# Begin of block attention: order of batch 1's rows, place of the value sums, and added products on TensorE

## Chip, core and metric

The kernel runs on one NeuronCore of one Trainium2 chip. The metric is the device time of one execution in microseconds (us); before the change the median of 3 runs is 1207.91 (1207.45 to 1208.69). Engines: PE is TensorE, DVE is VectorE, ACT is ScalarE, POOL is GpSimd, and SP issues most DMAs.

## The reference, cut to what matters

Four stages with residuals follow one another on x of shape (2, 1024, 128): a 16-head rotary attention, a routed layer of 8 experts, a block attention (16 heads of 8 features), and a gated mixing layer. The change lies at the border of the second and third stage.

```
x = x + experts(layernorm(x))                      # end of it: rows fetched back, added to x
h = layernorm(x)                                   # block attention
q, k, v = h @ Wq.T + bq, h @ Wk.T + bk, h @ Wv.T + bv     # 16 heads of 8
scores = q . k / sqrt(8);  where block(key) > block(query) the score is 0, not -inf   # blocks of 32
probs = softmax(scores);   ctx = probs @ v;        x = x + ctx @ Wo.T + bo
```

Since keys of later blocks have the score 0 and not minus infinity, they keep a weight in the softmax. The kernel adds their part with sums of v over later blocks ("suffix" sums).

## The kernel before

Each stage is a `Block`: five instruction streams, one for each engine, in an order written out by hand, with semaphores between them. A block ends when all five streams have ended, and the next one begins some 0.3 us later.

**End of `experts`.** SP fetches the sorted results back in four loads (`fetched[0..3]`). VectorE adds them to x, two loads first, then takes layer norm statistics of batch 0 and the variance (`var_ready`), then adds the other two loads. ACT takes the root. PE has no work after the last expert product.

**Projection block (inner block of `block_attention`).** Rows are normalized on VectorE (`take_rstd`, `normalize_rows`), turned on PE (`turn_normed`), copied by ACT (`keep_normed`). There are eight projections of 512 columns, `project(k)`: k 0 to 3 are q and k of batch 0, k 4 to 7 those of batch 1, each 128x512 f32. ACT keeps each with its bias (`keep_projected`). Each is split into a high part (fp32r) and a low part, the remainder (`low_part`, VectorE, which counts `stack_ready`). v is projected by `project_v(q)` and gets its bias on VectorE (`add_bias_v`). Between projections 5 and 6 PE takes the suffix sums of batch 0's values (`sum_values`: 12 products of 128x128, two instructions each in the trace), and the block's last VectorE work is `keep_sums`. SP stores the split q of the first heads after `stack_ready` 2 and k after 4, waits for each store to land, and loads them back in head layout (`load_pair`, `load_moving`, ten loads).

VectorE's order in this block, before:

```
take_rstd(0)  normalize_rows(0)  bq_scaled  stats, moments, var of batch 1
low_part 0, 1   take_rstd(1)  normalize_rows(1)   low_part 2, 3   add_bias_v 0, 1
low_part 4 .. 7 with add_bias_v 2, 3               keep_sums(batch 0)
```

**Attention block.** There are 8 groups of 4 heads (4 groups for each batch), 24 steps and 20 fills a group. A *fill* is `query_scores(f, 0)` and `(f, 1)`: two banks of up to 512 score columns (three banks rotate), of which VectorE takes row maxima (`row_max`, L1754) for the softmax shift. A *step* is `key_scores(j)` (scores with keys on partitions), exps on ACT, and, at every fourth step, value products (`values`) of step j-5. The lead is job -1: 22 fills without any step. At fill 12 PE turns the shifts of the first half (`shift_transposes`, 8 transposes), in order ahead of the fill's scores. `keep_out` on ACT (L1706) copies a half's sums at steps 10 and 26 of each group. Query and key scores have fp32r operands and 61 or 64 rows; everything else on PE is f32, which the engine multiplies in several passes.

## Time and profile before

| | us |
|---|---|
| median of 3 runs | 1207.91 |
| profiled execution, its own time | 1209.21 |
| its span, first to last instruction | 1207.1 |
| PE busy | 1080.6 (90%) |
| DVE busy | 931.7 (77%) |
| ACT busy | 695.9 (58%) |
| mean granted TensorE clock | 0.942 |

Times in the rows are microseconds from the start of the span. PE's busy time has pipelined ends in it, so that it can be full while the array streams less. PEclk is the granted share of 2.4 GHz: 0.50 is 1.2 GHz. In brackets behind a timeline row stands the idle time ahead of it and what ended it. L1234 is a line of the kernel.

### The profile page before, as it was taken

The numbers are of one execution on the slowest core, as the hardware profiler recorded it, in microseconds if no ns is written. First come the engines' busy times: TensorE is split into PE (matmuls) and PEld (weight loads), VectorE is DVE, ScalarE is ACT, GpSimd is POOL, SyncE is SP. The second block draws the span as 40 slices with busy tenths as digits, with TensorE's granted clock in tenths as the row PEclk, the third lists the DMA queues.
The fourth block names the chain that finished last, engine by engine and source line by source line (L and its number), as shares of the span: only waits on it lengthen the run. The fifth ranks groups of instructions, "written<-read, shape, count | busy, mean of one in ns | idle before, by whom it ended". The sixth has DMA issues, their size and how long they took to land. (4 is left out here: it accounts for less than half of the span.)

```text
span 1207.1 us, 33673 instructions
## 1 busy us (share of the span) xinstructions
PE 1080.6 (90%) x13115; PEld 623.6 (52%) x13115; DVE 931.7 (77%) x1453; ACT 695.9 (58%) x1324; POOL 363.8 (30%) x240
## 2 busy tenths in 40 slices
PE   3899999999999999999999984876899999999885
PEld 2345554554554555455455463863655654555443
DVE  6888888989888898898988885337857676666767
ACT  3567666676666766667666664643146564555652
POOL 0442552463354255246335422770000000000000
PEclk9999999999999999999999996896669999998998
DMA  6866665556555666555655554213533111110001
GB/s 177 224 146 147 151 140 142 136 132 163 139 136 129 150 151 138 144 139 129 160 139 140 129 152 139 60 51 94 168 123 124 48 33 44 48 54 20 1 2 35
DMA packets 65866, 138.14 MB, mean 114 GB/s; under 512 B 13217, under 2 KB 33602, under 8 KB 61714
## 3 DMA queue, kind: packets, MB, share of 16 engines
q1 hardware_dynamic: 63954, 132.87, 43.3%
q0 software_dynamic: 1856, 4.52, 1.3%
q8 instruction: 34, 0.56, 0.2%
q14 instruction: 22, 0.18, 0.0%
HBM read 62.77 MB, written 22.41 MB: 71 GB/s over the span
## 5 line engine op out<-in xcount | busy, mean ns | idle before, releaser
L482 ACT ACTIVATE a_probs<-a_score,a_negmax 128x1024 f32<-128x1024 f32 x256 | 285.2, 1114 | 247.3 <-DVE a_negmax L567 247.3
L567 DVE TENSOR_REDUCE a_negmax<-a_score 128x1 f32<-128x1024 f32 x256 | 309.6, 1209 | 90.6 <-PE a_score L362 90.1
L1754 DVE TENSOR_REDUCE a_lowest<-a_score 128x1 f32<-128x512 f32 (+3 forms) x320 | 181.8, 630 | 75.4 <-PE a_score L1558 37.7
L1700 ACT ACTIVATE a_probs_T<-a_score_T 128x1024 f32<-128x1024 f32 (+1 forms) x192 | 146.7, 810 | 136.6 <-PE a_score_T L1532 95.3
L328 POOL TENSOR_TENSOR residual<-residual,a_scaled 128x512 f32<-128x512 f32 x62 | 79.0, 1275 | 333.9 <-ACT a_scaled L494 333.9
L573 DVE STREAM_TRANSPOSE a_probs_Tb<-a_probs 128x1024 f32<-128x1024 f32 x128 | 156.9, 1226 | 0.1
L573 DVE STREAM_TRANSPOSE a_probs_Ta<-a_probs 128x1024 f32<-128x1024 f32 x128 | 156.9, 1226 | 0.0
L362 PE MATMUL a_score<-a_k_halvesa,a_q_twicea 64*128 64x512 f32 x512 | 142.0, 642 | 13.1 <-DMA a_k_halvesa<-a_k_turned 11.2
L362 PE MATMUL a_score<-a_k_halvesb,a_q_twiceb 64*128 64x512 f32 x512 | 140.5, 635 | 1.2 <-ACT a_probs L482 1.1
L374 PE MATMUL a_acc<-a_probs_Ta,a_v_repa 32*64 32x256 f32 x4096 | 131.0, 382 | 4.3 <-ACT a_scaled L494 3.9
L374 PE MATMUL a_acc<-a_probs_Tb,a_v_repb 32*64 32x256 f32 x4096 | 126.3, 380 | 1.8 <-ACT a_scaled L494 1.8
L374 PEld LDWEIGHTS a_acc<-a_probs_Ta,a_v_repa 32*64 32x64 f32 x4096 | 84.4, 131 | 76.3 <-issue 66.0
L374 PEld LDWEIGHTS a_acc<-a_probs_Tb,a_v_repb 32*64 32x64 f32 x4096 | 87.7, 131 | 58.4 <-issue 34.1
L1554 PE MATMUL a_score<-a_k_cur,a_q_still 61*128 61x512 f32 (+3 forms) x320 | 106.2, 434 | 6.9 <-DVE a_lowest L1754 5.3
L1497 POOL COPY a_v_pad<-a_v_den 128x288 f32<-128x288 f32 x8 | 3.6, 453 | 289.1 <-PE a_out L1579 289.1
L313 POOL TENSOR_TENSOR shared<-shared,a_tables 128x1024 f32<-128x1024 f32 x32 | 75.8, 2369 | 45.9 <-DMA shared<-shared 45.9
L1575 PE MATMUL a_out<-a_probs_T,a_v_pad 128*32 128x512 f32 (+3 forms) x768 | 82.1, 549 | 0.2 <-ACT a_probs_T L1700 0.2
L349 PE MATMUL a_acc<-a_xn_cur,a_w_cur 128*128 128x512 f32 x128 | 68.2, 634 | 10.3 <-ACT a_attn_T L488 10.3
L1532 PE MATMUL a_score_T<-a_q_moving,a_k_cur 61*128 61x512 f32 (+3 forms) x320 | 70.7, 392 | 7.1 <-ACT a_probs_T L1700 7.1
L314 POOL TENSOR_TENSOR shared<-shared,a_tables 128x1024 f32<-128x1024 f32 x32 | 75.8, 2368 | 0.0
L362 PEld LDWEIGHTS a_score<-a_k_halvesa,a_q_twicea 64*128 64x128 f32 x512 | 40.4, 187 | 64.2 <-issue 41.8
L1554 PEld LDWEIGHTS a_score<-a_k_cur,a_q_still 61*128 61x128 f32 x320 | 55.1, 206 | 34.0 <-DVE a_lowest L1754 25.9
(257 smaller groups left out, 1431.2 us busy)
## 6 DMA issues: line engine op xcount, KB each, us to landing
shared<-shared SPq DMA_DIRECT2D x136, 128.0 KB, 2.3
a_v_repa<-rows_v SPq DMA_DIRECT2D x64, 256.0 KB, 4.4
a_v_repb<-rows_v SPq DMA_DIRECT2D x64, 256.0 KB, 4.7
a_xn_cur<-normed_T SPq DMA_DIRECT2D x17, 512.0 KB, 3.3
rows_v<-a_v_stage SPq DMA_DIRECT2D x68, 128.0 KB, 2.4
a_q_twicea<-a_q_turned SPq DMA_DIRECT2D x32, 256.0 KB, 3.4
a_q_twiceb<-a_q_turned SPq DMA_DIRECT2D x32, 256.0 KB, 3.3
a_k_halvesa<-a_k_turned SPq DMA_DIRECT2D x32, 128.0 KB, 3.6
```

Of the source, the lines that this page charges most:

```text
L313: nc.gpsimd.tensor_tensor(raw[i][:], raw[i][:], tables[:, 0, :], ALU.mult).then_inc(rotated[i], 1)
L314: nc.gpsimd.tensor_tensor(rot[i][:], rot[i][:], tables[:, 1, :], ALU.mult).then_inc(rotated[i], 1)
L328: nc.gpsimd.tensor_tensor(rows, rows, scaled[j][:], ALU.add).then_inc(added, 1)
L362: last = nc.tensor.matmul(score_ps[s % 2][:, half * 512:half * 512 + 512], q_twice[h][rows, tile * P:tile * P + P], k_halves[h][rows, :], ...
L374: ins = nc.tensor.matmul(acc_ps[64 * c:64 * c + 64, a, 0:TB * 32], v_rep[h][rows, v_block, :], probs_T[h][rows, block_, :], start=i == 0, ...
L482: nc.scalar.activation(probs[s % 2][:], score_ps[s % 2][:], ACT.Exp, bias=negmax[:, s:s + 1], accum_out=den[:, s:s + 1]).then_inc(probs_re ...
L567: nc.vector.tensor_reduce(negmax[:, s:s + 1], score_ps[s % 2][:], axis=AX.X, op=ALU.max, negate=True)\
L573: nc.vector.transpose(out=probs_T[h][:, :, 32 * tile:32 * tile + 32], in_=probs[s % 2][:].rearrange("p (b k) -> p b k", b=KB))\
L1554: ins = nc.tensor.matmul(score_ps[n % 3][:, at:at + rest], q_still[m % 2][hp][rows, t * P:t * P + P], k_cur[m % 3][hp][rows, lo * P:lo * P ...
L1575: ins = nc.tensor.matmul(out_ps[32 * h:32 * h + 32, lo - 512 * half:512], v_pad[:, kt, h, :], probs_T[n % 4][:, h, 0:hi - lo], start=kt == ...
L1700: nc.scalar.activation(probs_T[k % 4][:, 2 * hp:2 * hp + 2, 0:hi - lo], score_T_ps[n % 2][:, :, 0:hi - lo], ACT.Exp).then_inc(pair_free, 1)
L1754: nc.vector.tensor_reduce(to, src, axis=AX.X, op=ALU.max, negate=True).then_inc(bank_free, 1)
```

## The change

- In `experts`, PE waits after the last expert product for the constants and the first load of rows, then issues six products of 256 columns (`keep_busy`) into a bank that nothing reads.
- In the projection block, batch 1's rows are normalized ahead of all lower parts, its root is taken before the kept projections, and its rows are turned ahead of `project_v` of batch 0. Two unread products stand behind the weight transposes and three behind the last `project_v`. The value sums and `keep_sums` leave this block.
- In the attention block, the lead's first six fills carry two parts of the value sums each, into the bank of the outputs; the other sixteen carry one unread product of 256 columns each. VectorE keeps the sums after fill 7, and the first value products wait for that.

```
--- before.py
+++ after.py
@@ -837,6 +837,10 @@
                     if j == 0:
                         pe.wait_ge(w2_loaded, 16)
                     out_of(j, expert(j))
+                pe.wait_ge(operands.fixed_loaded, 16)
+                pe.wait_ge(fetched[0], 16)
+                for _ in range(6):
+                    operands.keep_busy(rank_ps[:, 0:256])
 
             @block.scalar
             def _(act):
@@ -998,6 +1002,10 @@
         sp.dma_start(self.bv_b[:], row(bv).broadcast_to([P, D])).then_inc(self.bias_loaded, 16)
         sp.dma_start(self.bo_row[:], row(bo)).then_inc(self.bias_loaded, 16)
 
+    def keep_busy(self, to):
+
+        self.nc.tensor.matmul(to, self.fixed[:, 0:P], self.fixed[:, 0:256], start=True, stop=True)
+
     def take_stats(self, x, b):
 
         for t in range(b * TB, b * TB + TB):
@@ -1071,14 +1079,15 @@
                 twice = parts[i][part][rows, cols].bitcast(F32).rearrange("p (r n) -> p r n", r=1).broadcast_to([rows.stop - rows.start, 2, N])
                 queue.dma_start(to, twice).then_inc(stored, 16)
 
-        def sum_values(to, b):
-
-            for half in range(2):
-                for kt in range(4 * half, TB):
-                    off = min(kt - 4 * half, 4)
-                    ins = nc.tensor.matmul(to[:, half * P:half * P + P], fixed[:, off * P:off * P + P], v_den[:, b, kt, :, 0:DH1],
-                                           start=kt == 4 * half, stop=kt == TB - 1)
-            return ins
+        SUM_PARTS = [(half, kt) for half in range(2) for kt in range(4 * half, TB)]
+
+        def sum_part(to, b, half, kt):
+
+            off = min(kt - 4 * half, 4)
+            return nc.tensor.matmul(to[:, half * P:half * P + P], fixed[:, off * P:off * P + P], v_den[:, b, kt, :, 0:DH1],
+                                    start=kt == 4 * half, stop=kt == TB - 1)
+
+        keep_busy = operands.keep_busy
 
         def keep_sums(src, b):
 
@@ -1129,7 +1138,6 @@
             xn = sb2("xn", [P, T, D])
             moments, var, root = operands.moments, operands.var, operands.root
             rstd, newton = sb2("rstd", [P, T]), sb2("newton", [P, T])
-            sums_ps = ps2("sums", [P, 512])
             s_ps = [ps2(f"s{i}", [P, 512]) for i in range(DEPTH)]
             v_ps = [ps2(f"v{i}", [P, 512]) for i in range(2)]
             turned_ps = [v_ps[0], v_ps[1], w_ps, s_ps[0]]
@@ -1137,7 +1145,7 @@
             bias_scaled = sem("bias_scaled")
             proj_ready, full_ready, stack_ready = (sem(n) for n in ("proj_ready", "full_ready", "stack_ready"))
             high_ready = [sem("even_high_ready"), sem("odd_high_ready")]
-            v_ready, v_added, sums_ready = sem("v_ready"), sem("v_added"), sem("sums_ready")
+            v_ready, v_added = sem("v_ready"), sem("v_added")
             first_loaded = operands.first_loaded
             ORDER = [(i, 2 * b + c) for b in range(B) for i in range(2) for c in range(2)]
 
@@ -1189,22 +1197,22 @@
                         ins.then_inc(v_ready, 1)
 
                     transpose_weights(pe)
+                    for _ in range(2):
+                        keep_busy(s_ps[3][:, 0:256])
                     turn_normed(0)
                     pe.wait_ge(wT_copied, 1)
                     for k in range(4):
                         project(k)
+                    turn_normed(1)
                     for q in range(2):
                         project_v(q)
-                    turn_normed(1)
                     pe.wait_ge(xT_kept, 4)
                     for k in range(4, 2 * DEPTH):
                         project(k)
-                        if k == 5:
-                            pe.wait_ge(operands.fixed_loaded, 16)
-                            pe.wait_ge(v_added, 2)
-                            sum_values(sums_ps, 0).then_inc(sums_ready, 1)
                         if k >= 6:
                             project_v(k - 4)
+                    for _ in range(3):
+                        keep_busy(w_ps[:, 0:256])
 
                 @block.scalar
                 def _(act):
@@ -1227,10 +1235,9 @@
                     keep_weights(act)
                     keep_normed(0)
                     act.wait_ge(bias_scaled, 1)
+                    operands.take_root(act, 1)
                     for k in range(4):
                         keep_projected(k)
-                        if k == 1:
-                            operands.take_root(act, 1)
                     keep_normed(1)
                     for k in range(4, 2 * DEPTH):
                         keep_projected(k)
@@ -1283,11 +1290,9 @@
                     step(operands.take_stats(core.x, 1))
                     step(operands.take_moments(1))
                     operands.take_var(1).then_inc(operands.var_ready, 1)
-                    for k in range(2):
-                        low_part(k)
                     take_rstd(1)
                     normalize_rows(1)
-                    for k in range(2, 4):
+                    for k in range(4):
                         low_part(k)
                     for q in range(2):
                         add_bias_v(q)
@@ -1295,9 +1300,6 @@
                         low_part(k)
                         if k >= 6:
                             add_bias_v(k - 4)
-                    dve.wait_ge(operands.suffix_cleared, 1)
-                    dve.wait_ge(sums_ready, 1)
-                    keep_sums(sums_ps, 0)
 
 
         GROUPS = B * G
@@ -1326,7 +1328,8 @@
         pair_filled, pair_free = sem("pair_filled"), sem("pair_free")
         capped_ready, halves_ready, shift_ready, shift_kept = sem("capped_ready"), sem("halves_ready"), sem("shift_ready"), sem("shift_kept")
         pv_done, out_copied, rden_ready, main_cleared, pad_cleared, v_padded = (sem(n) for n in ("pv_done", "out_copied", "rden_ready", "main_cleared", "pad_cleared", "v_padded"))
-        SUMS_AT = 40
+        SUMS_AT, SUM_FILLS = 40, 6
+        sums_ready, sums_kept = sem("sums_ready"), sem("sums_kept")
         QUARTERS = B * N // 512
         WEIGHTS_AT, FRONT, TURN_X = 168, (167, 168, 187, 203), (171, 175, 190, 204)
         KEYS, RECEPTANCE, VALUES = (174, 178, 194, 205), (174, 178, 197, 205), (177, 181, 203, 206)
@@ -1567,6 +1570,8 @@
                     pe.wait_ge(pair_free, pair["scores", m * STEPS + 2 * kq + 1] + 1)
                     if kq == 0:
                         pe.wait_ge(v_padded, m + 1)
+                        if m == 0:
+                            pe.wait_ge(sums_kept, 1)
                         if m == G:
                             pe.wait_ge(bank_free, bank["sums"] + 1)
                     if kt == 0 and (m or half):
@@ -1646,7 +1651,15 @@
                 def sum_later_values():
                     n = bank["sums"]
                     pe.wait_ge(bank_free, n - 2)
-                    sum_values(score_ps[n % 3], 1).then_inc(bank_filled, 1)
+                    for half, kt in SUM_PARTS:
+                        ins = sum_part(score_ps[n % 3], 1, half, kt)
+                    ins.then_inc(bank_filled, 1)
+
+                def sum_two_parts(i):
+                    for half, kt in SUM_PARTS[2 * i:2 * i + 2]:
+                        ins = sum_part(out_ps, 0, half, kt)
+                    if i == SUM_FILLS - 1:
+                        ins.then_inc(sums_ready, 1)
 
 
                 for j in JOBS:
@@ -1658,6 +1671,10 @@
                         if f < GROUPS * FILLS:
                             query_scores(f, 0)
                             query_scores(f, 1)
+                            if f < SUM_FILLS:
+                                sum_two_parts(f)
+                            elif j < 0:
+                                keep_busy(score_T_ps[1][:, 0, 0:256])
                     if j % 4 == 1 and live(j - 5):
                         for k in range(2):
                             values((j - 5) // STEPS, (j - 5) % STEPS // 2 + k)
@@ -1798,6 +1815,11 @@
                     dve.wait_ge(bank_filled, n + 1)
                     rows = core.x[:, m // G * TB + 4 * half:m // G * TB + 4 * half + 4, :]
                     nc.vector.tensor_tensor(rows, score_ps[n % 3][:].rearrange("p (t d) -> p t d", t=4), rows, ALU.add).then_inc(bank_free, 1)
+
+                def keep_early_sums():
+                    dve.wait_ge(operands.suffix_cleared, 1)
+                    dve.wait_ge(sums_ready, 1)
+                    keep_sums(out_ps, 0).then_inc(sums_kept, 1)
 
                 def keep_later_sums():
                     n = bank["sums"]
@@ -1907,6 +1929,8 @@
                         if f < GROUPS * FILLS:
                             row_max(f, 0)
                             row_max(f, 1)
+                        if f == SUM_FILLS + 1:
+                            keep_early_sums()
                         if columns_at(f):
                             shift_columns(*columns_at(f))
                     if j == SUMS_AT:
```

## Rows read from the trace of the kernel before

**Rows 1.** The page's 40 slices: granted TensorE clock, in tenths of full speed.

```profile
PEclk9999999999999999999999996896669999998998
```

**Rows 2.** Half-microsecond windows: busy us (instructions) of each engine, PEclk, DMA share, GB/s.

```profile
830.50:831.00 0.50, 0.50 (x2) 0.30 (x1) 0.00 (x0) 0.47 (x2) 0.00 (x0) 0.51 0.00 0
851.00:851.50 0.50, 0.43 (x5) 0.39 (x5) 0.50 (x3) 0.00 (x0) 0.50 (x2) 0.97 0.41 131
895.50:896.00 0.50, 0.50 (x8) 0.08 (x4) 0.16 (x1) 0.00 (x0) 0.00 (x0) 0.66 0.21 82
```

**Rows 3.** Windows of lead, steps 2 to 9, and the same steps of group 1.

```profile
850.18:878.64 28.46, 27.30 (x102) 19.87 (x103) 25.45 (x53) 2.52 (x4) 2.34 (x5) 0.52 0.53 168
880.50:898.06 17.56, 17.20 (x103) 10.22 (x103) 9.03 (x20) 7.51 (x13) 0.00 (x0) 0.56 0.48 181
921.74:932.85 11.11, 10.37 (x89) 5.78 (x89) 8.94 (x22) 5.85 (x10) 0.00 (x0) 1.00 0.30 96
```

**Rows 4.** Timeline of PE (start us, us, what, count, [idle before]), projections to first scores.

```profile
837.87 3.64 PE L1181 MATMUL a1p_s_ps<-normed_T,a1p_w_T 128*128 128x512 f32 x4 [0.69 <-ACT normed_T L1214]
841.34 2.84 PE L1079 MATMUL a1p_sums_ps<-a_v_den,a_fixed 128*128 128x128 f32 x24
844.01 1.02 PE L1181 MATMUL a1p_s_ps<-normed_T,a1p_w_T 128*128 128x512 f32 x2
844.88 1.05 PE L1187 MATMUL a1p_v_ps<-a1p_w_T,normed_T 128*128 128x128 f32 x8
...
850.18 0.44 PE L1558 MATMUL a_score<-a_k_cur,a_q_still 64*128 64x128 f32 x4 [2.50 <-PEq L1144]
```

**Rows 5.** Timeline of VectorE, end of the experts' block to end of projections.

```profile
816.75 2.19 DVE L957 SCALAR_TENSOR_TENSOR residual<-f_y_rows,f_p_max,residual 128x128 f32<-128x128 f32 x8 [8.06 <-DMA f_y_rows<-slots_y]
...
821.41 2.18 DVE L957 SCALAR_TENSOR_TENSOR residual<-f_y_rows,f_p_max,residual 128x128 f32<-128x128 f32 x8
...
829.41 0.17 DVE L1016 TENSOR_SCALAR a_n_var<-a_n_moments 128x8 f32<-128x8 f32 x1
...
833.28 0.20 DVE L1251 RECIPROCAL a1p_rstd<-a_n_root 128x8 f32<-128x8 f32 x1
...
836.38 0.68 DVE L1272 TENSOR_TENSOR a_k_lo<-a1p_full,a_k_hi 128x512 fp32r<-128x512 f32 x1
...
849.40 0.48 DVE L1087 TENSOR_TENSOR a_suffix<-a1p_sums_ps,a_fixed 128x128 f32<-128x128 f32 x2
```

**Rows 6.** Timeline of SP's DMA issues in the projection block.

```profile
838.16 0.35 SPq L1072 DMA_DIRECT2D rows_k<-a_k_hi  x1
...
842.24 0.77 SPq L1094 DMA_DIRECT2D a_k_cur<-rows_k  x2
...
844.90 1.82 SPq L1094 DMA_DIRECT2D a_q_moving<-rows_q  x4
```

**Rows 7.** Timeline of ACT: kept projections, first exps, copies of a half's sums.

```profile
830.15 0.69 ACT L1221 ACTIVATE a1p_full<-a1p_s_ps,a1p_bq_scaled 128x512 f32<-128x512 f32 x1 [1.26 <-PE a1p_s_ps L1181]
...
833.59 0.67 ACT L1221 ACTIVATE a1p_full<-a1p_s_ps,a_b_col 128x512 f32<-128x512 f32 x1
...
878.59 2.73 ACT L1700 ACTIVATE a_probs_T<-a_score_T 128x1024 f32<-128x1024 f32 x3 [10.43 <-PE a_score_T L1532]
...
898.06 0.59 ACT L1706 ACTIVATE normed_T<-a_out 128x512 f32<-128x512 f32 x1
...
932.85 0.59 ACT L1706 ACTIVATE normed_T<-a_out 128x512 f32<-128x512 f32 x1
```

**Rows 8.** Groups by line in the lead, 850.18 to 878.64.

```profile
L1754 DVE TENSOR_REDUCE a_lowest<-a_score 128x1 f32<-128x512 f32 (+3 forms) x44 | 24.4, 623 | 3.2 <-PE a_score L1554 1.6 <-PE a_score L1558 1.6
...
L1558 PE MATMUL a_score<-a_k_cur,a_q_still 64*128 64x128 f32 x41 | 11.3, 351 | 2.5 <-PEq L1144 2.5
```

**Rows 9.** Timeline of VectorE in the lead, behind the first shift transposes.

```profile
866.39 9.18 DVE L1754 TENSOR_REDUCE a_lowest<-a_score 128x1 f32<-128x512 f32 x16 [1.61 <-PE a_score L1554]
```

**Rows 10.** Timeline of PE: the first value products of group 0.

```profile
887.07 3.21 PE L1575 MATMUL a_out<-a_probs_T,a_v_pad 128*32 128x512 f32 x16
```

More of the change, by code:

```diff
@@ L839, in _ @@
                     out_of(j, expert(j))
+                pe.wait_ge(operands.fixed_loaded, 16)
+                pe.wait_ge(fetched[0], 16)
+                for _ in range(6):
+                    operands.keep_busy(rank_ps[:, 0:256])
             @block.scalar
@@ L1191, in _ @@
                     transpose_weights(pe)
+                    for _ in range(2):
+                        keep_busy(s_ps[3][:, 0:256])
                     turn_normed(0)
@@ L1648, in sum_later_values, with sum_two_parts @@
                     pe.wait_ge(bank_free, n - 2)
-                    sum_values(score_ps[n % 3], 1).then_inc(bank_filled, 1)
+                    for half, kt in SUM_PARTS:
+                        ins = sum_part(score_ps[n % 3], 1, half, kt)
+                    ins.then_inc(bank_filled, 1)
+                def sum_two_parts(i):
+                    for half, kt in SUM_PARTS[2 * i:2 * i + 2]:
+                        ins = sum_part(out_ps, 0, half, kt)
+                    if i == SUM_FILLS - 1:
+                        ins.then_inc(sums_ready, 1)
                 for j in JOBS:
@@ L1800, in add_projected, with keep_early_sums @@
                     nc.vector.tensor_tensor(rows, score_ps[n % 3][:].rearrange("p (t d) -> p t d", t=4), rows, ALU.add).then_inc(bank_free, 1)
+                def keep_early_sums():
+                    dve.wait_ge(operands.suffix_cleared, 1)
+                    dve.wait_ge(sums_ready, 1)
+                    keep_sums(out_ps, 0).then_inc(sums_kept, 1)
                 def keep_later_sums():
@@ L1909, in _ @@
                             row_max(f, 1)
+                        if f == SUM_FILLS + 1:
+                            keep_early_sums()
                         if columns_at(f):
```

45 lines of the change are left out of this document (22 added, 23 removed).

## The prediction

> **What bounds the kernel now.** I read first the page's slices: the granted clock is at nine tenths or more nearly everywhere and at six tenths in slices 28 to 30, which cover the last step of the routed layer and the begin of block attention [rows 1]. The half-microsecond windows put the edges: TensorE is at 1.2 GHz until 831.0 us and without a break from 851.5 to 895.8 us [rows 2]; two products at 837.87 that take 3.64 us show it at half clock there too [rows 4]. Those 44 us hold the lead (22 fills: the query scores whose row maxima VectorE takes) and the first ten steps.
>
> In the lead, 850.18 to 878.64, both are nearly full: VectorE 25.45 of 28.46 us, PE 27.30 [rows 3]. PE's "busy" counts pipelined ends, so I go by gaps: the row maxima sum to 24.4 us with only 3.2 us idle before them [rows 8], and one gap of 1.61 is behind the slow transposes [rows 9]. The lead is VectorE's; the clock costs it some 2 us.
>
> The first steps are PE's: 880.50 to 898.06 is 17.56 us with PE busy for 17.20 and VectorE for 9.03; the same eight steps of the next group, 921.74 to 932.85, take 11.11 us at 2.4 GHz [rows 3]. Both windows go from about the scores of step 2 to the copy of the half's sums, and hold two pairs of value products each; ACT's rows show their ends [rows 7].
>
> The projection block (823.9 to 849.9) is a relay of short waits. Its last work is `keep_sums` on VectorE, ending 849.88 [rows 5], and PE begins the next block 0.3 us later after 2.50 us of idleness [rows 4]. SP issues its last load there until 846.72 [rows 6]: 3.2 us of slack, not more.
>
> **The change, part by part.**
>
> *Six products in the experts' end.* They start when the first rows are back, when VectorE begins at 816.75 [rows 5]. A 512-column product (two instructions in the trace) costs 1.82 us at 1.2 GHz (3.64 for two) and 0.87 at 2.4 (844.01 to 844.88) [rows 4], so 256 columns are 0.91 or 0.43: six are 5.5 us at most, done by 822.3. VectorE needs this block until 823.6 (821.41 and 2.18) [rows 5]. Cost 0; without that cover it would be 5.5. The two products after the weight transposes, 1.8 us at worst, reach 826.8; the first half of batch 0's rows is ready at about 826.0 (block start 823.9, and half of the 3.1 us below plus the small steps). 0.7 late, but the second half of the rows comes 1 us behind and ACT's first kept projection has a later wait (next). Cost 0 to 0.5; I take 0.
>
> *Batch 1's rows ahead of the lower parts.* The variance is ready at 829.58 [rows 5], the root thus about 829.9. The five small steps and the normalization take 3.1 (833.28 to 836.38) [rows 5]: the rows are ready by 833.0 instead of 836.4. ACT holds its first projection for the root until 829.95, where before it began at 830.15, after the slow first product: nothing lost. It ended the fourth at 834.26 (833.59 and 0.67) [rows 7], with the root among them, and now ends it at 833.85. PE turns the rows at 832.1 to 833.6, ACT keeps them by 835.0 (two copies of 0.6), project_v of batch 0 fills PE until 835.4, and projection 4 starts there instead of at 837.87 [rows 4], at 2.4 GHz if the clock rose and PE had no gap.
>
> From projection 4's start to VectorE's end it was 12.0 us (837.87 to 849.88). Of this the value sums' place on PE goes (841.34 to 844.01, 2.7, the next product's start in the list), `keep_sums` 0.5 [rows 5], and the half clock on two products 1.7 [rows 4]: 7.1 us are left, so VectorE ends at 842.5.
>
> But then SP is late next. The third and fourth lower part took 1.75 (836.38 to the keys' store at 838.16, less its 0.03) [rows 5, 6], so four after 833.0 end at 836.5, against 838.13. From there SP needed 8.6 us: the keys' stores, their landing (the keys' loads begin at 842.24), ten load issues until 846.72 [rows 6]. That gives 845.1. The query stores are now handed over at 834.8, only 1.7 us ahead of the keys' (before 4.8), so both share the DMA engines; I allow 0.7. SP ends at 845.8, the block after it starts at 846.1 instead of 850.18: **-4.1 us** (3.3 to 5.1).
>
> PE is out of work at 840.5, its three products last to 841.8, and then it waits some 4 us for SP. That gap is longer than the 2.5 us after which the clock fell at 851.5 [rows 2, 4]. So I expect the fall again, and the lead begins at 1.2 GHz.
>
> *Value sums in the lead.* 12 products of 128 columns took 2.84 us at 2.4 GHz [rows 4], 0.22 each; the double at half clock, 0.9 per fill for the first six fills. The scores of these six are 32 matmuls, most of 128 columns, whose mean is 351 ns with their pipelined ends [rows 8]; I estimate 0.23 for each without, 7.4 us at half clock, beside 6 of row maxima. With the sums (5.1) PE needs 12.5 at half clock, 6.5 at full. If the clock rises 4 to 5 us into the lead, the six fills take 4.3 and two thirds of 6.9, 8.9; before they took 7.1, the ends of VectorE's 6 and its first waits. `keep_early_sums` adds 0.5 to VectorE. **+2.3.**
>
> *One 256-column product per fill, 16 times.* The scores of a fill cost PE 0.43 to 0.5 us at 2.4 GHz, and the product 0.43: 0.9 against VectorE's 1.15 (sixteen row maxima in 9.18 us [rows 9]). Hidden behind VectorE at full clock; at half clock PE has 1.8 and the cover is gone, +0.65 per fill. At full clock the eight transposes shrink from 1.7 to 0.85 and the 1.61 gap closes; 1.1 with what else is idle there: **-1.1.** The lead thus costs +1.2 (from -1 with no slow start to +4).
>
> Here a rule bears on it: the Trainium skill, page "TensorE: Matmul & The Clock Gate", Part 3, says that matmuls start and end strictly in program order, so an unread product cannot step aside for the scores behind it. This case's trace agrees: the scores behind the eight transposes left VectorE idle for 1.61 us [rows 9]. By the rule alone, at half clock for the whole lead, the products would be paid in full (rival 1); if the clock rises they lie in VectorE's time.
>
> *First steps.* With 2.4 GHz they should look like the later group: 17.56 less 11.11 is 6.45, plus 0.2 for steps 0 and 1, where ACT's exps set the pace (2.73 for three [rows 7]): **-6.6** (0 if the clock has fallen).
>
> Sum: -4.1 + 2.3 - 1.1 - 6.6 = -9.5. The profiled execution's own time is 1209.21 (span 1207.1); it gives 1199.7. The median of the runs is 1.3 under it: **1198.4 us**. SP's later queue moves with it and has slack: the first shift is placed long before step 8, and group 1's loads 20 us ahead.
>
> **Why the clock should rise.** It rose at 831.0 during full 128-row products back to back, and at 895.8 in value products mixed with scores; from 851.5 on it stayed down although PE was always "busy", with 61-row scores only, spaced by VectorE [rows 2, 3]. The new stream is back-to-back at half clock, half of it full four-pass products. The stretch from 887 to 892, which has value products too (3.21 us of them) and stayed slow [rows 10], speaks against it. [...]
>
> On when it rises, the Trainium skill (same page, Part 1) says the place varies between runs of one kernel. One trace cannot show this; taken alone the slow start would be anything from none to twice mine, 1196 to 1201.
>
> **Rivals.**
> 1. *The products make PE the bound* (8%, the other side): the clock stays down. Lead: 12.5 for six fills, 16 times 1.8, 1.7 of transposes, 43.0 instead of 28.5: +14.5, less 4.1, nothing back in the first steps: 1218.3. With a later rise it decides at about 11 us of lag, that is most of the lead at half clock. For it: 44 slow microseconds and the stretch 887 to 892.
> 2. *Late or broken rise* (20%): up only after the sixth fill, 1201.5; after the fourteenth (+4.6 more), about 1206; a second fall in the lead with the first steps partly slow, the same region. Center 1204.
> 3. *The projection gives nothing* (8%): SP, or ACT held for the root, takes the 4.1 back; the clock works: 1202.5.
> 4. *No fall between the blocks* (6%): no slow start, 1195 to 1196.
>
> **Chances and range.** Forecast 58%, own range 1195.5 to 1201.5. Until no more than two in ten are out: 1194.5 to 1206. A measurement of this kernel tells about 0.2% (2.4 us) from no change: faster is under 1205.5, which has the forecast, rivals 3 and 4 and most of 2: 0.83; same 0.07 (the end of 2); slower 0.10 (rival 1 and a little).
>
> **What the profile will show.** Right: the second block starts near 846 with SP the last of the first; projection 4 near 835.4; PEclk 0.5 for 3 to 6 us of the lead and 1.0 from there through 890; row maxima of fills 6 to 21 without gaps; the copy of the first sums near 888.5 instead of 898.06. Wrong: PEclk 0.5 through the lead with row maxima spaced by 0.9 us each; VectorE, not SP, ending the projection block; or later groups that get longer and eat the gain.

## The result, and the profile after

The changed kernel takes 1219.99 us (median of 4 runs, 1219.11 to 1223.74), the kernel before 1208.3 on the same runs: ratio 1.0102, 95% interval 1.0078 to 1.0125. It is slower by 11.7 us where 9.5 less were forecast. The profiled execution's own time is 1219.58.

The page of the changed kernel: span, and granted clock by slices.

```profile
span 1217.8 us, 33781 instructions
...
PEclk9899999999999999999999995888688989999997
```

The mean clock is 0.942 in both profiles. Slices 25 to 33 read 6 8 9 6 6 6 9 9 9 before [rows 1] and 5 8 8 8 6 8 8 9 8 now. The loss of clock has been spread, not removed. I cut the span where the work changes hands: from the end of the experts' block to PE's first score (*projection block*), to ACT's first exps (*lead*), to the first copy of a half's sums (*first steps*), and the rest.

| us | to experts' end | projection block | lead | first steps | rest | span |
|---|---|---|---|---|---|---|
| before | 823.59 | 26.59 | 28.41 | 19.47 | 309.04 | 1207.1 |
| before, a second profile | 824.07 | 26.70 | 28.34 | 19.53 | 306.26 | 1204.9 |
| changed | 826.66 | 23.22 | 37.75 | 17.70 | 312.47 | 1217.8 |
| changed, a second profile | 823.95 | 23.23 | 37.76 | 19.46 | 310.90 | 1215.3 |

**Projection block.** SP's timeline of the changed kernel in this block:

```profile
837.86 0.64 SPq L1080 DMA_DIRECT2D rows_q<-a_q_hi  x1
...
839.52 0.35 SPq L1080 DMA_DIRECT2D rows_k<-a_k_hi  x1
...
842.27 1.30 SPq L1103 DMA_DIRECT2D a_q_still<-rows_q  x2
844.96 0.77 SPq L1103 DMA_DIRECT2D a_k_cur<-rows_k  x2
...
847.63 1.81 SPq L1103 DMA_DIRECT2D a_q_moving<-rows_q  x4
849.83 0.58 SPq L1080 DMA_DIRECT2D rows_q<-a_q_hi  x1
```

PE's timeline there:

```profile
838.50 2.74 PE L1189 MATMUL a1p_s_ps<-normed_T,a1p_w_T 128*128 128x512 f32 x6
...
843.72 1.46 PE L1007 MATMUL a1p_w_ps<-a_fixed 128*128 128x256 f32 x6
849.88 0.69 PE L1561 MATMUL a_score<-a_k_cur,a_q_still 64*128 64x128 f32 x4 [4.70 <-PEq L1152]
```

VectorE's:

```profile
834.03 2.14 DVE L1267 TENSOR_SCALAR a1p_xn<-residual,a_n_moments,a1p_rstd 128x128 f32<-128x128 f32 x8
...
845.10 0.68 DVE L1283 TENSOR_TENSOR a_v_den<-a1p_v_ps,a_bv_b 128x512 f32<-128x512 f32 x1
```

Batch 1's rows are normalized from 834.03 on, ahead of the lower parts. Projection 4 starts at 838.50, 11.8 us after the experts' end, as forecast (835.4 less 823.6). VectorE ends at 845.78. SP ends at 849.44, 0.4 us ahead of the next block: the bound has passed to SP, which had 3.2 us of slack before [rows 6]. PE has its last three products done at 845.2 and waits 4.70 us.

**Lead and first steps.** Windows of the changed kernel: the lead, the first steps, and inside the lead the first six fills, six fills with products ahead of the shift's transposes, and the fills behind them.

```profile
849.88:887.63 37.75, 37.63 (x156) 23.93 (x158) 26.65 (x55) 2.47 (x3) 2.34 (x5) 0.67 0.43 135
887.63:905.33 17.70, 16.40 (x115) 9.70 (x111) 10.04 (x22) 9.31 (x13) 0.00 (x0) 0.71 0.48 180
849.88:862.12 12.24, 12.24 (x61) 9.96 (x61) 6.41 (x12) 0.00 (x0) 2.34 (x5) 0.50 0.90 282
862.12:872.50 10.38, 10.38 (x26) 4.77 (x25) 7.94 (x18) 0.00 (x0) 0.00 (x0) 0.50 0.32 103
875.06:886.40 11.34, 11.22 (x54) 6.75 (x52) 11.03 (x24) 1.88 (x2) 0.00 (x0) 1.00 0.12 38
```

The clock is at 0.50 up to the transposes and at 1.00 behind them. PE has no idle time while it is at 0.50; VectorE works 6.41 of 12.24 us and 7.94 of 10.38. PE's timeline in that stretch, scores (L1557) and unread products (L1007) in turn:

```profile
863.27 0.69 PE L1557 MATMUL a_score<-a_k_cur,a_q_still 61*128 61x384 f32 x2
...
864.00 1.22 PE L1007 MATMUL a_score_T<-a_fixed 128*128 128x256 f32 x2
865.15 0.79 PE L1557 MATMUL a_score<-a_k_cur,a_q_still 61*128 61x512 f32 x2
865.87 1.22 PE L1007 MATMUL a_score_T<-a_fixed 128*128 128x256 f32 x2
867.02 0.79 PE L1557 MATMUL a_score<-a_k_cur,a_q_still 61*128 61x512 f32 x2
```

A fill takes 1.87 us from its scores to the next fill's (863.27, 865.15, 867.02): 0.73 of scores and 1.15 with the product and the load of the next weights. VectorE's timeline shows the price as idle time in the brackets:

```profile
852.81 1.29 DVE L1771 TENSOR_REDUCE a_lowest<-a_score 128x2 f32<-128x512 f32 x2 [1.47 <-PE a_score L1561]
...
860.44 1.29 DVE L1771 TENSOR_REDUCE a_lowest<-a_score 128x2 f32<-128x512 f32 x2 [1.44 <-PE a_score L1561]
...
871.60 1.29 DVE L1771 TENSOR_REDUCE a_lowest<-a_score 128x1 f32<-128x512 f32 x2 [0.59 <-PE a_score L1557]
875.17 9.42 DVE L1771 TENSOR_REDUCE a_lowest<-a_score 128x1 f32<-128x512 f32 x16 [2.28 <-PE a_score L1557]
```

Before, that idle time was 3.2 us in the whole lead [rows 8], with one gap of 1.61 [rows 9]; now up to 1.47 us pass ahead of an early fill's pair, 0.59 ahead of a later one's, and 2.28 at the transposes. ACT's first exps and first copy of sums, which answer to [rows 7]:

```profile
887.63 2.72 ACT L1717 ACTIVATE a_probs_T<-a_score_T 128x1024 f32<-128x1024 f32 x3 [10.68 <-PE a_score_T L1535]
...
905.33 0.59 ACT L1723 ACTIVATE normed_T<-a_out 128x512 f32<-128x512 f32 x1
```

### The profile page after: what moved, and what is told of

The parts are those of the page before. It is cut to its first block and busy times, and to the rows that moved or that the text cites. A ratio compares the mean times of both kernels' runs of the same rounds, so it can differ in the third digit from the quotient of the medians.

```text
span 1217.8 us, 33781 instructions
## 1 busy us (share of the span) xinstructions
PE 1097.3 (90%) x13169; PEld 631.2 (52%) x13169; DVE 932.8 (77%) x1453; ACT 695.9 (57%) x1324; POOL 363.7 (30%) x240
## 5 line engine op out<-in xcount | busy, mean ns | idle before, releaser
L362 PE MATMUL a_score<-a_k_halvesa,a_q_twicea 64*128 64x512 f32 x512 | 142.0, 642 | 13.1 <-DMA a_k_halvesa<-a_k_turned 11.2
L1557 PE MATMUL a_score<-a_k_cur,a_q_still 61*128 61x512 f32 (+3 forms) x320 | 96.9, 418 | 6.0 <-DVE a_lowest L1771 4.4
L1580 PE MATMUL a_out<-a_probs_T,a_v_pad 128*32 128x512 f32 (+3 forms) x768 | 85.0, 565 | 0.2 <-ACT a_probs_T L1717 0.2
L349 PE MATMUL a_acc<-a_xn_cur,a_w_cur 128*128 128x512 f32 x128 | 68.1, 633 | 10.3 <-ACT a_attn_T L488 10.3
L1557 PEld LDWEIGHTS a_score<-a_k_cur,a_q_still 61*128 61x128 f32 x320 | 49.4, 198 | 34.3 <-DVE a_lowest L1771 24.5
```

Of the source, the lines that this page charges most:

```text
L362: last = nc.tensor.matmul(score_ps[s % 2][:, half * 512:half * 512 + 512], q_twice[h][rows, tile * P:tile * P + P], k_halves[h][rows, :], ...
L1557: ins = nc.tensor.matmul(score_ps[n % 3][:, at:at + rest], q_still[m % 2][hp][rows, t * P:t * P + P], k_cur[m % 3][hp][rows, lo * P:lo * P ...
L1580: ins = nc.tensor.matmul(out_ps[32 * h:32 * h + 32, lo - 512 * half:512], v_pad[:, kt, h, :], probs_T[n % 4][:, h, 0:hi - lo], start=kt == ...
```

## The experiments

The kernel before ran again beside each of four groups (e1 to e4; c0, c1, e5, e6; e7 to e10; e11 to e13), and each ratio is against it. In e1 to e4 and e7 to e10 the experts' block ends at 839 to 844 us in every profile, not at 824 to 828, so that the kernel before takes 1228 to 1229 there. What lengthens the routed layer in these two groups is open: no edit touches it. I go by the length of each stage, taken as above. The rest of the span (behind the first copy of sums, code that no experiment touches) ranges from 305.1 to 315.7 over the profiles; what that means is told below.

| us | projection block | lead | first steps | sum of the three | rest | ratio (95% interval) |
|---|---|---|---|---|---|---|
| before, two profiles | 26.6, 26.7 | 28.4, 28.3 | 19.5, 19.5 | 74.5, 74.6 | 309.0, 306.3 | |
| changed, two profiles | 23.2, 23.2 | 37.8, 37.8 | 17.7, 19.5 | 78.7, 80.5 | 312.5, 310.9 | 1.0102, 1.0107 |
| e1 no lead products | 23.2 | 34.0 | 18.4 | 75.6 | 305.1 | 1.0028 (0.9995 to 1.0061) |
| e2 sums back | 23.9 | 32.1 | 16.1 | 72.1 | 305.9 | 1.0003 (0.9969 to 1.0036) |
| e3 lead as before | 23.8 | 28.3 | 17.6 | 69.7 | 315.7 | 0.9988 (0.9953 to 1.0023) |
| e4 lead products alone | 26.9 | 32.2 | 16.1 | 75.1 | 305.8 | 1.0001 (0.9971 to 1.0031) |
| e5 bridge | 24.2 | 28.9 | 18.0 | 71.2 | 309.4 | 0.9985 (0.9951 to 1.0020) |
| e6 bridge, sums back | 24.4 | 32.6 | 17.8 | 74.7 | 312.5 | 1.0030 (0.9997 to 1.0063) |
| e7 bridge, steps | 23.2 | 29.1 | 18.9 | 71.3 | 312.3 | 0.9991 (0.9956 to 1.0026) |
| e8 512 columns | 24.9 | 37.6 | 14.6 | 77.1 | 309.0 | 1.0001 (0.9969 to 1.0033) |
| e9 bridge, no lead products | 24.3 | 32.5 | 19.5 | 76.3 | 309.1 | 1.0039 (1.0011 to 1.0067) |
| e10 order alone | 23.2 | 28.7 | 18.4 | 70.2 | 305.8 | 0.9954 (0.9922 to 0.9986) |
| e11 the same again | 23.2 | 28.5 | 20.5 | 72.2 | 315.4 | 0.9994 (0.9958 to 1.0029) |
| e12 moving later | 22.3 | 28.9 | 16.2 | 67.4 | 309.4 | 0.9953 (0.9922 to 0.9984) |
| e13 all fills | 23.5 | 28.5 | 16.1 | 68.1 | 312.4 | 0.9971 (0.9940 to 1.0001) |

### e1, e2, e3, e4: parts of the change undone, one part alone

e1 takes the sixteen unread products out of the lead:

```diff
                             if f < SUM_FILLS:
                                 sum_two_parts(f)
-                            elif j < 0:
-                                keep_busy(score_T_ps[1][:, 0, 0:256])
```

> The changed kernel without the sixteen unread products in the lead; everything else of the change stays. Theory 1 (at half clock PE pays for all that was put in the lead, in full): the lead, first score to first exps, falls from 37.75 us to about 33 (the first six fills, with the value sums, stay near 12; the rest goes at VectorE's pace of about 1.25 us a fill), the clock stays at half until the value products, and the first exps to the first copy of sums takes about 19.5: 1217 us. Theory 2 (the products are hidden, and the time is lost outside the lead, ahead of and behind the block's begin): no change within 2 us, 1218 to 1220.

The lead took 34.0 us, 3.7 less. The clock stayed at half for 48 us, through the transposes too, and the first steps took 18.4. Theory 1 holds for the lead. The 3.7 us are a net price: in the changed kernel six of the products ran at half clock and ten at full.

e2 puts the value sums back into the projection block:

```diff
                     for k in range(4, 2 * DEPTH):
                         project(k)
+                        if k == 5:
+                            pe.wait_ge(operands.fixed_loaded, 16)
+                            pe.wait_ge(v_added, 2)
+                            for half, kt in SUM_PARTS:
+                                ins = sum_part(sums_ps, 0, half, kt)
+                            ins.then_inc(p_sums_ready, 1)
...
-                            if f < SUM_FILLS:
-                                sum_two_parts(f)
-                            elif j < 0:
+                            if j < 0 and f >= SUM_FILLS:
```

> The changed kernel with batch 0's value sums and their keeping back in the projection block, behind projection 5; the sixteen lead products stay. Theory 1: the lead loses about 5 us of PE work in its first six fills (to about 32), the projection block gains at most 1 (SP ends it, so the sums lie in its slack): about 1216 us. Theory 2: no change within 2 us.

The lead took 32.1, 5.6 less. The clock was at half for 17 us of it, not 25, so the 5.6 are not the sums' work alone. The projection block took 0.7 more, and that is one issue of SP: the first two loads of the keys took 1.47 us where they took 0.77 in the changed kernel. e10, with the sums in the block and 0.77 there, takes 23.2. So the sums themselves are free there, in the slack that SP leaves.

e3 is e1 and e2 together, so that of the change only the projection block and the products outside the lead stand.

> Only the change outside the lead: six, two and three products and batch 1's rows first; sums and lead as before. Theory 1: the projection block keeps 2.5 to 3.4 us of gain and the lead takes 28.4 as before, so 1205.5 us if the 3.07 us ahead of the changed code and the 3.3 us behind step 10 are not part of the change. Theory 2: both stay, 1211 to 1212.

The three stages took 69.7 us, 4.8 less than before; the lead is 28.3 again. The ratio 0.9988, whose interval includes 1, doesn't show it; in the profile the rest, 315.7 us and the longest of all, takes it back.

e4 is the kernel before with the sixteen products alone:

```diff
                             query_scores(f, 0)
                             query_scores(f, 1)
+                            if j < 0 and f >= 6:
+                                operands.keep_busy(score_T_ps[1][:, 0, 0:256])
```

> The kernel before with nothing but one unread 256-column product behind each of the fills 6 to 21. Theory 1: at half clock 0.9 us each, of which VectorE's slack hides a third: lead +6 to +9 us, 1214 to 1217 us; if the clock rises within the lead, less. Theory 2: within 1 us of the kernel before.

The lead grew by 3.8 us, the first steps shrank by 3.4, since the clock had come back within the transposes, 17 us after its fall, and stayed up until 7 us into the first steps. The products pay for themselves and no more; the forecast of 6 to 9 in the lead was too high. Windows of the stretch from the transposes to the first exps, in e1 (no products) and in e4:

```profile
888.20:901.10 12.90, 12.48 (x46) 9.44 (x46) 11.76 (x25) 2.47 (x3) 0.00 (x0) 0.50 0.15 43
...
888.00:901.00 13.00, 12.88 (x65) 7.67 (x65) 11.90 (x25) 2.47 (x3) 0.00 (x0) 1.00 0.13 43
```

The same transposes stand ahead of both. So they don't bring the clock back by themselves; the products have a part in it.

### c0, c1: both kernels once more

> The kernel before once more. The ledger of the first two profiles has 3.07 us ahead of the changed code and 3.3 us behind step 10 that the change does not touch. If they are a matter of the execution and not of the change, this profile's stage of the routed layer and its later groups (first copy of sums to the last) move by as much from the first profile of the same kernel, while the projection block (26.6 us) and the lead (28.4 us) stay.

> The changed kernel once more, beside the kernel before on one chip. Theory 1 (the lead pays, the rest is the execution's): projection block 23.2 us, lead 36 to 38, first steps 17 to 20, so slower by 4 to 5 us, ratio 1.003 to 1.004. Theory 2 (the whole 11.7 us is the change's): ratio 1.0095.

The windows of the kernel before: projection block, lead, first steps, rest.

```profile
824.07:850.77 26.70, 21.17 (x93) 13.72 (x93) 18.12 (x63) 11.04 (x19) 0.74 (x3) 0.79 0.39 98
850.77:879.11 28.34, 27.18 (x102) 19.74 (x103) 25.34 (x53) 2.47 (x3) 2.33 (x5) 0.52 0.53 168
879.11:898.64 19.53, 18.89 (x112) 11.36 (x110) 10.10 (x23) 9.42 (x13) 0.00 (x0) 0.56 0.45 163
898.64:1204.90 306.26, 269.28 (x2200) 152.09 (x2200) 209.48 (x496) 165.52 (x237) 3.17 (x7) 0.95 0.13 40
```

The same four of the changed kernel:

```profile
823.95:847.18 23.23, 17.41 (x79) 11.31 (x79) 17.56 (x61) 10.39 (x19) 0.74 (x3) 0.88 0.40 101
847.18:884.94 37.76, 37.64 (x156) 23.97 (x158) 26.64 (x55) 2.47 (x4) 2.33 (x5) 0.66 0.43 134
884.94:904.40 19.46, 18.03 (x115) 10.11 (x111) 10.04 (x22) 9.23 (x14) 0.00 (x0) 0.65 0.44 164
904.40:1215.30 310.90, 273.77 (x2200) 153.18 (x2200) 209.47 (x496) 165.56 (x237) 3.18 (x7) 0.94 0.13 40
```

The 3.07 us ahead of the changed code (826.66 and 823.59 in the first two profiles) are gone (823.95 and 824.07), so they were the execution's. The stages repeat to 0.1 us, save the first steps. The ratio is 1.0107 again (1.0033 to 1.0181), while the three stages give only 5.9 us. The rest is 4.6 us longer at a mean clock of 0.94 against 0.95, with the same instructions.

### e5, e6, e9: a bridge of products over PE's wait

e5 has twelve products behind the last projection in place of three:

```diff
-                    for _ in range(3):
+                    for _ in range(12):
                         keep_busy(w_ps[:, 0:256])
```

> The changed kernel with twelve unread products, not three, behind the last projection: they reach over PE's wait for SP (843.7 to 849.9). Theory A (the lead's products can hold the 2.4 GHz but not bring it back, and the clock was lost in that wait): no fall at the border, lead 27 to 29 us with VectorE as its pace, first steps about 14, 8 to 10 us less than the changed kernel. Theory B (the lead's stream is too thin at either level): the clock falls within the lead all the same, lead 33 to 36.

Windows of e5, the three stages:

```profile
823.59:847.82 24.23, 21.21 (x97) 15.17 (x97) 17.56 (x60) 10.29 (x19) 0.74 (x3) 0.93 0.38 97
847.82:876.74 28.92, 28.62 (x156) 18.45 (x158) 25.99 (x55) 2.47 (x4) 2.34 (x5) 1.00 0.55 175
876.74:894.77 18.03, 16.45 (x115) 9.65 (x111) 10.05 (x22) 9.23 (x13) 0.00 (x0) 0.72 0.48 176
```

The clock is at 1.00 through the whole lead, which takes 28.92 us where the same instructions took 37.76: 8.8 us from nine products on an idle engine. In total e5 takes 1206.2 us where the changed kernel took 1220.95 beside it, 14.7 less; against the kernel before its ratio is 0.9985, no difference. That is the cause of the longer lead, shown in one edit: the changed lead is PE's at half clock and VectorE's at full. But 28.92 is no better than the 28.3 of the lead before, which went at half clock; and the clock fell 1.8 us into the first steps, which took 18.0 us where about 14 were expected.

e6 is e2 with eight products in the bridge.

> The same with the value sums back behind projection 5 and eight products behind the last projection. Theory A: lead 27 us, first steps 14, from the experts' end to the first copy of sums 65 us (74.5 before). Theory B: the clock falls at the lead's first fills, which have scores only, and comes back with the eight transposes: 70 to 72 us.

The clock fell 2.9 us into the lead, in fills that carry scores only, and came back 17 us later at the transposes. Lead 32.6: theory B, where no product stands. But the three stages took 74.7 us, not 70 to 72, and gained nothing on the kernel before.

e9 is e5 without the sixteen lead products.

> The bridge (twelve products) with the value sums in the first six fills, but none of the sixteen lead products. If these hold the clock, it falls here within 3.5 to 7 us after the sixth fill (from about 855 us) and the rest of the lead and the first steps go at half clock: lead 29 to 30, first steps 19. If the bridge alone does it, both are as with the sixteen products (28.9 and 18.0) or shorter.

Windows of e9: the lead up to the fall, and behind it.

```profile
863.61:865.50 1.89, 1.89 (x18) 1.63 (x19) 0.94 (x3) 0.00 (x0) 1.89 (x4) 1.00 0.78 269
865.59:896.15 30.56, 29.51 (x110) 20.85 (x109) 25.07 (x53) 2.47 (x3) 0.38 (x1) 0.50 0.48 148
```

It fell 2.0 us into the lead, earlier than the missing products could matter; with the same bridge, the same wait of 1.8 us behind it and the same first fills e5 had kept it. The lead took 32.5 us, not 29 to 30. So e9 doesn't show that the sixteen products hold the clock. It does show that a bridge with 1.8 us of waiting behind it doesn't always do.

### e7, e8: more products in the steps, larger ones in the lead

e7 has eleven in the bridge, and one behind the key scores of steps 0 to 4:

```diff
                     if live(j):
                         key_scores(j)
+                        if j < 5:
+                            keep_busy(out_ps[:, 0:256])
```

> The changed kernel with eleven unread products behind the last projection, and one more of 256 columns behind the key scores of each of the steps 0 to 4. With the bridge alone the clock held through the lead and fell at its end, 1.8 us into the first steps. Theory A (a stream with the products holds the 2.4 GHz): no fall until the value products, first steps 14 to 15 us instead of 18.0, so 3 us under the bridge kernel there. Theory C (the steps' waits for the exps let it fall whatever is added): first steps 18 to 21, since the products then cost PE 0.9 us each at half clock.

The lead held the clock again (29.1). It fell 0.6 us ahead of the first exps, came back 6.8 us later, and the steps took 18.9 where e5's took 18.0 with 10.3 us at half clock. The five products cost at least what the clock gave. Theory C's side.

e8 is e4 with products of 512 columns.

> The kernel before with one unread product of 512 columns, not 256, behind each of the fills 6 to 21. The 256-column ones left the clock at half until the shift's transposes. [...] Theory E (scores between the products keep it down whatever their size): half clock until the transposes, lead 28.4 plus 16 times 1.4, less what VectorE hides: 43 to 48.

Windows of e8: four fills at half clock ahead of the rise, and the fills behind it.

```profile
871.30:882.20 10.90, 10.90 (x19) 3.36 (x18) 5.19 (x12) 0.00 (x0) 0.00 (x0) 0.50 0.66 211
883.80:901.80 18.00, 18.00 (x77) 7.79 (x78) 13.76 (x27) 2.47 (x3) 0.00 (x0) 1.00 0.10 31
```

The clock came back at 883.4, 12.1 us after the first of these products (871.3), and 1.8 us ahead of the transposes; the lead took 37.6, under the 43 to 48 of theory E, which had the clock at half until the transposes. A rise at fill 8 or 9, and a lead of 31 to 33 us with it, did not come either. Two things follow. The transposes aren't needed for the rise. And the larger products brought it no sooner: with 256 columns it came 11.7 us behind the first product in e4 (876.18 to 887.9) and 17.1 us after the fall, as here. They only cost more until then. With the clock at full, the first steps took 14.6; the prediction had 12.9 for them (19.5 less 6.6).

### e10, e11, e12, e13: the order alone, and what ends the block

e10 has batch 1's rows and root first and its rows turned ahead of `project_v`, no unread product anywhere, sums and lead as before. e11 is the same kernel again.

> The order of the projection block alone: batch 1's rows first, its root first, its rows turned ahead of project_v; no unread product anywhere, sums and lead as before. If the order gives the projection block's gain: from the experts' end to the first score 24 to 25 us (26.6 before, 23.2 with the whole change), total 2 us under before. If the products outside the lead give it: 26 to 26.6.

> The order of the projection block alone once more, on whichever chip this is. If its gain (ratio 0.9954, 4.2 us from the experts' end to the first copy of sums) is its own and not the execution's: ratio 0.995 to 0.998 again, projection block 23.2 us, lead 28.4 to 28.7.

Windows of e10, projection block and rest:

```profile
842.10:865.28 23.18, 18.72 (x93) 12.79 (x93) 17.97 (x63) 10.66 (x19) 0.75 (x3) 0.86 0.40 100
912.33:1218.10 305.77, 267.58 (x2200) 151.52 (x2200) 209.59 (x496) 165.47 (x237) 3.17 (x7) 0.96 0.13 40
```

The same of e11:

```profile
827.51:850.73 23.22, 18.90 (x92) 12.91 (x93) 17.97 (x63) 10.82 (x19) 0.74 (x3) 0.84 0.40 103
...
899.68:1215.10 315.42, 278.57 (x2201) 154.14 (x2200) 209.91 (x497) 165.55 (x237) 3.19 (x7) 0.92 0.13 39
```

The projection block is 23.2 us both times, as with all products: the whole of its 3.4 us comes from the order, and the eleven products outside the lead add nothing to it. The ratios are 0.9954 and 0.9994; the second misses the 0.995 to 0.998 that I expected, and its interval includes 1. So the order's gain is shown in the block, and on the total in one run of two. One kernel, one code, and a rest of 305.8 and 315.4 us, at a mean clock of 0.96 and 0.92: single executions scatter by 10 us behind the stages.

e12 is e5 with eleven products and SP's loads of the moving queries in the next block:

```diff
                     load_pair(sp, k_cur[0], k_rows, 0, 1, first_loaded[1])
-                    load_moving(sp, 0)
...
+                load_moving(sp, 0)
                 sp.wait_ge(q_stored[1], STORED)
                 load_still(sp, 1)
```

> The bridge kernel (eleven products behind the last projection) with SP's four loads of group 0's moving queries put at the head of the next block. If SP ends the projection block, as the traces of the changed kernel say, it ends 1.5 us earlier (22.7 instead of 24.2), the lead stays 29: ratio 0.997 against the kernel before. If the border is PE's or VectorE's, no change.

Windows of e12, the three stages:

```profile
825.99:848.27 22.28, 20.65 (x95) 14.59 (x95) 17.57 (x60) 10.29 (x19) 0.74 (x3) 0.92 0.37 93
848.27:877.17 28.90, 28.60 (x156) 18.46 (x158) 26.00 (x55) 2.47 (x3) 2.33 (x5) 1.00 0.59 185
877.17:893.36 16.19, 14.10 (x115) 7.58 (x111) 10.04 (x22) 9.11 (x13) 0.00 (x0) 0.89 0.52 191
```

The block is 1.9 us shorter than e5's, but not all of this comes from the moved loads. SP's issue of the first key loads in e5, and in e7, which has the eleven products of e12:

```profile
841.89 1.76 SPq L1103 DMA_DIRECT2D a_k_cur<-rows_k  x2
...
857.94 0.77 SPq L1103 DMA_DIRECT2D a_k_cur<-rows_k  x2
```

e7's block takes 23.2 us, and it is the one to compare with: the moved loads gave 0.9 us, not the 1.5 expected. That shows that SP ended the block there. In e12 PE ends it:

```profile
843.05 4.91 PE L1007 MATMUL a1p_w_ps<-a_fixed 128*128 128x256 f32 x22
848.27 0.44 PE L1561 MATMUL a_score<-a_k_cur,a_q_still 64*128 64x128 f32 x4 [0.30 <-PEq L1152]
```

The bridge lasts until 847.96, and SP was done at 846.90, so the bridge itself now costs about 1 us. With 67.4 us for the three stages e12 is the shortest, and by the runs it is faster than the kernel before: 1202.08 against 1208.17 us, ratio 0.9953 (0.9922 to 0.9984). The order alone had the same ratio once (e10). The first steps took 16.2 us, not e5's 18.0, with the same instructions on PE: the clock fell at 884.0, 6.8 us into them, and was back 3.4 us later.

e13 has the order, six products in the bridge, one behind each of all 22 fills, sums in the projection block.

> Order of the projection block, six unread products behind the last projection, and one 256-column product behind each of all 22 fills; the value sums stay in the projection block. If a stream with products holds the clock once it has it: no fall in the lead, which is then VectorE's alone, 26.5 to 27.5 us, first steps 18 (the clock falls where the products end), 70 us from the experts' end to the first copy of sums. If the short waits at the border let it fall all the same: lead 38 to 42.

Windows of e13:

```profile
826.01:849.50 23.49, 21.31 (x105) 14.91 (x105) 17.96 (x62) 10.72 (x19) 0.74 (x3) 0.85 0.41 101
849.50:878.00 28.50, 28.24 (x144) 17.15 (x146) 25.61 (x53) 2.47 (x4) 2.33 (x5) 1.00 0.56 176
878.00:894.08 16.08, 13.92 (x115) 7.57 (x111) 10.04 (x22) 9.10 (x13) 0.00 (x0) 0.89 0.52 191
```

The clock holds through the lead at 1.00, and still the lead takes 28.5 us, as before at 0.52 [rows 3], where 26.5 to 27.5 were expected. The first steps take 16.1, less than the 18 expected, since the clock fell only 6.2 us into them. The ratio, 0.9971, has 1 just inside its interval.

## Why the prediction was wrong, point by point

**The bound, read rightly.** The lead of the kernel before was VectorE's, the first steps PE's at half clock. At full clock throughout (e8) they take 14.6 us: 4.9 less than 19.5, three quarters of the 6.6 forecast. So this term would have been 1.7 us too large even with the clock up.

**Six products in the experts' end, two behind the transposes: 0 forecast.** They ran in PE's wait, and e10, which has none, ends the block as early. Right.

**Projection block: -4.1 forecast, -3.4 measured**, inside the bounds' lower edge of 3.3. The order, the passing of the bound to SP (e12) and PE's wait (4 us forecast, 4.70 measured) were right. SP's path from the keys' store to the last load was forecast at 8.6 and 0.7 for sharing, and took 9.9: the keys' loads could begin 5.4 us after the keys' first store (839.52 to 844.96), before 4.1 [rows 6]. The fall of the clock in the wait was forecast too.

**The step that failed: "If the clock rises 4 to 5 us into the lead".** It rose after 25.1 and 25.4 us in the two profiles. PE was without a gap all that time, and about half of it was full products. The prediction gives no row for its 4 to 5 us. From back-to-back products in the block before, and from the rise in value products at 895.8, I took it that a dense stream would bring the clock back. The stretch from 887 to 892 [rows 10] said otherwise, and I had noted it as speaking against and left it 8% (rival 1) and 20% (rival 2) of the chance. Holding and regaining turned out to be different things. With the clock at full on entry, the lead's stream kept it for 29 us (e5, e7, e12, e13). From half clock the mix of scores and lead products did bring it back, but late: 11.7 to 13.1 us behind the first of these products in six profiles (both of the changed kernel, e2, e4, e6, and e8 with products twice as large), which is 17 to 27 us behind the fall. Without lead products the fall lasted 37.6 to 47.8 us in all seven profiles (both of the kernel before, e1, e3, e9, e10, e11), through the same transposes, and in e1 through the value sums as well. So the step had the direction right and the time wrong: 25 us into the lead, not 4 to 5. What sets that time I can't say.

From that one step the terms followed. The lead: +1.2 forecast, +9.4 measured (value sums about 5.6 by e2, lead products 3.7 by e1, both measured by leaving them out, each with the change in the clock's course that it brings). That is rival 1's mechanism, PE as the bound, in the place and near the size given for its early part: the first fills took 12.24 us, where 12.5 was worked out for half clock, and a fill with a product 1.87, where it was 1.8. Its end, the clock at half throughout, did not come; the fills behind the transposes ran at full clock. That the rival's total, 1218.3, lies within 2 us of the result is luck: its lead was 5 us too long, and it has none of the time lost behind the first steps. The first steps: -6.6 forecast, -1.8 and -0.1 measured, for the clock fell again 1.0 and 1.3 us into them. That is not simply the end of the products: e12 and e13 kept it for 6.8 and 6.2 us there.

**The term -1.1 for the lead at full clock was wrong as well, and the clock's course doesn't excuse it.** e5 and e13 have the full clock and need 28.9 and 28.5 us. VectorE works for 26.0 (0.5 of it keeping the sums) and 25.6 of them, and is idle for 2.9 in both, against 3.0 before [rows 3]. The gap behind the transposes did shrink, from 1.61 to 0.73 us in e5; others grew. That the products fill what the faster clock frees on PE is my reading; no run has the full clock through the lead without them. In these runs the lead's products are at best neutral in the lead, and their gain is the first steps.

**The rest: 0 forecast.** In the profiles it is 3.4 and 4.6 us longer than the kernel before's, pair by pair, and the runs say 11.7 and 11.8 in all, of which the three stages give 4.2 and 5.9. The later groups hold the same instructions; their length goes with the granted clock in them (0.96: 305.8, 0.95: 306.3, 0.94: 310.9, 0.92: 315.4). So 3.4 and 4.6 us of the result lie in clock lost later. The medians differ by another 4.1 and 1.3 us, which these stages don't place. That a late start of the first group brings this about in the changed kernel, and not in e2 or e4 (305.9 and 305.8), was not shown. It stays open.

**The rule of program order.** That PE takes products in program order, and so an unread one delays the scores behind it, was the right one to weigh: each of the six that ran at half clock delayed them by 1.15 us. The other ten ran at full clock, behind the transposes, at VectorE's pace. It was no rule against the change at full clock, where e5 shows VectorE almost fed.

## What to carry to other kernels

Work put on an engine "to keep its clock up" is priced at the low clock first: if it stands in order ahead of work that another engine waits for, it costs double exactly when it is needed. Put it where the engine has nothing behind it (e5's nine more products in a wait took 8.8 us off the lead and 14.7 off the runs, the sixteen in the stream cost 3.7 of lead by e1), size it to reach the end of the wait and not past it, and look for who ends the wait (e12: four loads moved, 0.9 us, and then the bridge was the one that ended the block, 1 us behind the loads). And measure a reordering apart from its filler: here the order alone had the projection block's whole gain.

## What the runs showed of the hardware

- The granted clock stayed at 1.2 GHz for 25 us with PE never idle (changed kernel, 849.88 to 875.0). In the experts' block of the same profile six back-to-back products, 4.73 us from 819.93 on, had it at 2.4 GHz before they ended.
- Scores with one unread product per fill kept it at 2.4 GHz for 29 us (e5, e7, e12, e13). From 1.2 GHz the same kind of stream raised it 11.7 to 13.1 us behind its first product, with 256 columns or 512, with the transposes ahead of the rise or behind it (e8).
- The same kernel's later groups took 305.8 and 315.4 us in two profiles, at mean clocks of 0.96 and 0.92 with the same instructions. Stage lengths, not totals, told these experiments apart.
